# Two fused graph-attention layers: layer 0's softmax bound on ScalarE, its shift as a reduction, and another order of the mixed phase

## The chip, the cores and the metric

One core of a Trainium2 chip runs the whole program. The metric is the time of one execution on the device, in microseconds (us). A kernel's time is the median of several executions. Profiles come from one execution of their own.

## The reference, cut to what matters

For each of 16 graphs with 512 nodes and 256 channels, layer 0 is one attention head with a 0/1 mask and layer 1 has eight heads whose logits get the logarithm of the clipped adjacency:

```python
# layer 0
q = x @ Wq + bq;  k = x @ Wk + bk
scores = where(adj == 0, -1e18, (q @ k.T) / sqrt(256))
attn   = where(adj == 0, 0, softmax(scores))
x = layernorm(x + (attn @ x) @ Wc) * gamma + beta
# layer 1, heads of 32 channels
logits = q_h @ k_h.T / sqrt(32) + log(clip(adj, 1e-8))
x = layernorm(x + concat_h(softmax(logits) @ v_h) @ Wo.T + bo) * gamma + beta
```

## The kernel before, in words

Each graph goes through a front (layer 0 and layer 1's projections), a back (layer 1's attention) and a tail (output projection, residual, layernorm, store). The program runs phases: in phase i the front of graph i+1, the back of graph i and the tail of graph i-1 are mixed. There are 18 phases: one with a front only, one with front and back, fourteen full ones (a hardware loop), one with back and tail, one with the tail alone. In layer 1 a "quad" is four heads by 128 keys; a back has eight quads of two pairs each.

The order inside a phase is a list written out by hand, `SCHEDULE` for the mixed phases (`FIRST` and `LAST` for the ends). Every engine walks the same list and does its own share of each named stage (function `follow`), so PE, VectorE (`dve`), ScalarE (`act`) and GpSimd (`pool`) each have a strict queue, and semaphores tie them. SyncE issues all transfers in an order of its own, with waits on VectorE's and GpSimd's progress.

Stages that the change and the prediction touch:

- `max0` (L650, L652, L989): upper bounds of layer 0's scores on PE; VectorE takes the negated maximum of 512 columns per row tile, into `mx0`.
- `u` (L608, L826): PE forms x @ Wc and, in one more column, what the key's bias adds to each row's scores; ScalarE copies it to `U`. `floor` (L995) adds a large constant to that column for the four row tiles, on VectorE, into `floor0`: a bound for rows without any neighbour.
- `shift0` (L1000): VectorE takes the smaller of `mx0` and `floor0`, 4 numbers per partition, into `nm0`. ScalarE spreads it to `NM0` (L832), and PE adds it in the first `scores0` (L667).
- `reciprocal`, `normalise` (L1057), `high_output` (L862, ScalarE), `low_output` (L1061, VectorE): turn the sums of one group of four heads into the high and low parts `OTH`, `OTL` of the attention's output. With index 1 they belong to the graph before. `project` (L770) on PE multiplies them by Wo; its sixth matmul is the first that reads `OTL` of group 1. `project` on VectorE (L1070) adds the residual; `stats1`, `norm1` (L1086) and `output` make the layernorm.
- `scores1` (L719, L847, L1144): PE's scores of a pair, ScalarE's exponential, and GpSimd's multiplication by the clipped adjacency (the "mask"; a few are on VectorE, stages `mask`, L985). `values1`, `denominators1` (L742) sum a quad on PE after its masks.
- `residual` (L1127, L1129): two GpSimd operations that prepare `res` from `xn`; `norm0` (L1044) on VectorE overwrites `xn` and waits for them, `transpose` on PE (L685) waits for `norm0`.
- `max1` (L698, L1005): one matmul and one VectorE reduction per head and row tile. `clip` (L973), `bias` (L977): VectorE makes the clipped adjacency and the mask of missing edges.

The four `MISC` banks of PSUM are given out in the list's order to the stages of `MISC_DRAIN`; a fill waits until the use four places before it has been drained. `skip_back` and `skip_front` are places in that count with no work.

Of the kernel before, what the change touches and what calls it, by code (L numbers as in the profile page):

```python
# [32 lines left out]
ALU = mybir.AluOpType  # L33
ACT = mybir.ActivationFunctionType
AX = mybir.AxisListType

P = 128
# [13 lines left out]
class Phase:  # L51
# [20 lines left out]

SCHEDULE = [
    ("reciprocal", 1, 0), ("max1", 1, 0), ("split", 0), ("split", 1), ("reciprocal", 1, 1),
# [13 lines left out]
    ("reciprocal", 0, 0), ("reciprocal", 0, 1), ("scores1", 6, 0), ("transpose", 0), ("scores1", 6, 1),  # L88
    ("transpose", 1), ("reciprocal", 0, 2), ("reciprocal", 0, 3), ("values1", 5), ("scores1", 7, 0),
# [6 lines left out]
]  # L96

LAST = [
# [129 lines left out]
def two_layer_graph_attention(nc, x, x_t, adj_t, wq0, wk0, wc0, wq1_t, wk1_t, wv1_t, wo1_t,  # L228
                              channel_cols, channel_rows, out):
    B, N, D = x.shape  # L230
    T = N // P
# [15 lines left out]
    with ExitStack() as ctx:  # L247
        def sb(name, shape, dt=F32):
            return ctx.enter_context(nc.sbuf_tensor(name, shape, dt))
# [4 lines left out]
        def sem(name):  # L254
            return ctx.enter_context(nc.semaphore(name))
# [27 lines left out]
        absent = sb("absent", [P, 1])  # L283
        Q0H, Q0L = (sb(n, [P, C, N], F32R) for n in ("Q0H", "Q0L"))
        U = sb("U", [P, T, 1 + D + 2])
        mx0 = sb("mx0", [P, T])
        floor0 = sb("floor0", [P, T])
        nm0 = sb("nm0", [P, T])
        floor_bias = sb("floor_bias", [P, 1])
        NM0 = sb("NM0", [P, T, P], F32R)  # L290
# [72 lines left out]
        floor0_ready = sem("floor0_ready")  # L363
        nm0_ready = sem("nm0_ready")
# [20 lines left out]
        sums_out = sem("sums_out")  # L385
# [16 lines left out]
        def misc_bank(ph, *stage):  # L402
            return MISC[misc.bank(ph, *stage)]

        def wait_drained(eng, ph, *stage):

            e = MISC_DRAIN[stage[0]]
            eng.wait_ge(misc_drained[e], misc.count(ph, e, *stage))

        def wait_filled(eng, ph, *stage):  # L410
            eng.wait_ge(misc_filled, misc.count(ph, "fill", *stage))
# [376 lines left out]
        def _(act):  # L788
# [23 lines left out]
            def hi(ph, stage, c, dst, bias):  # L812

                wait_filled(act, ph, stage, c)
                act.activation(dst[:, c, :], misc_bank(ph, stage, c)[:], ACT.Identity,
                               bias=cols[:, bias, c:c + 1]).then_inc(hi_written, 1)
# [7 lines left out]
            def context_rows(ph, t):  # L824
                wait_filled(act, ph, "u", t)
                act.copy(U[:, t, 1:1 + D + 2], misc_bank(ph, "u", t)[:, 0:D + 2]).then_inc(misc_drained["act"], 1)  # L826

            def shift0(ph):

                act.wait_ge(nm0_ready, ph.j + 1)  # L830
                for t in range(T):
                    act.activation(NM0[:, t, :], ident[:], ACT.Identity, scale=nm0[:, t:t + 1]).then_inc(nm0_spread, 1)  # L832
# [31 lines left out]
            def xn_high(ph, c):  # L864
# [4 lines left out]
            do = {  # L869
                "prepare": prepare, "split": split,  # L870
                "q0": lambda ph, c: hi(ph, "q0", c, Q0H, BQ0),
                "u": context_rows, "shift0": shift0,
                "scores0": exp0, "transpose": xn_high,
                "q1": lambda ph, c: hi(ph, "q1", c, Q1H, BQ1),
                "k1": lambda ph, c: hi(ph, "k1", c, K1H, BK1),
# [8 lines left out]
        def _(dve):  # L884
# [76 lines left out]
            def lo(ph, stage, c, dst, hi_part, bias):  # L961

                wait_high(ph, stage, c)
                dve.scalar_tensor_tensor(out=dst[:, c, :], in0=misc_bank(ph, stage, c)[:],  # L964
                                         scalar=cols[:, bias, c:c + 1], in1=hi_part[:, c, :].bitcast(F32),
                                         op0=ALU.add, op1=ALU.subtract).then_inc(misc_drained["dve"], 1)
# [19 lines left out]

            def max0(ph, t):
                wait_filled(dve, ph, "max0", t)
                dve.tensor_reduce(mx0[:, t:t + 1], misc_bank(ph, "max0", t)[:], AX.X,  # L989
                                  ALU.max, negate=True).then_inc(misc_drained["dve"], 1)  # L990

            def floor(ph):

                wait_drained(dve, ph, "u", T - 1)
                dve.tensor_scalar(floor0[:], U[:, :, 1 + D], floor_bias[:, 0:1], None, ALU.add).then_inc(floor0_ready, 1)  # L995

            def shift0(ph):
                wait_drained(dve, ph, "max0", T - 1)
                dve.wait_ge(floor0_ready, ph.j + 1)
                dve.tensor_tensor(nm0[:], mx0[:], floor0[:], ALU.min).then_inc(nm0_ready, 1)  # L1000

            def max1(ph, g, n):
                t, h = divmod(n, PER_GROUP)
# [79 lines left out]
            def norm1(ph):  # L1083
# [5 lines left out]
            do = {  # L1089
                "prepare": prepare, "split": split, "clip": clip, "bias": bias,  # L1090
                "q0": lambda ph, c: lo(ph, "q0", c, Q0L, Q0H, BQ0),
                "mask": mask, "max0": max0, "floor": floor, "shift0": shift0, "context0": context0,
                "stats0": stats0, "norm0": norm0, "stats1": stats1,
                "transpose": xn_low,
                "q1": lambda ph, c: lo(ph, "q1", c, Q1L, Q1H, BQ1),
# [98 lines left out]
```

## Time and profile before

| | us |
|---|---|
| median of 3 runs (lowest, highest) | 1311.65 (1310.07, 1313.34) |
| the profiled execution, its span | 1313.88, 1312.1 |
| PE busy | 1188.1 (91%) |
| VectorE busy | 1019.7 (78%) |
| GpSimd busy | 733.7 (56%) |
| ScalarE busy | 522.1 (40%) |

Busy times add up an engine's instructions; the idle rest of an engine is waiting for another one or for its own next instruction. In the timeline an instruction's duration includes time in which it has been started but is held up. Matmuls overlap each other, so their starts say more than their ends. Successive VectorE instructions overlap by 0.08 us in the records, and successive GpSimd ones by 0.04.

### The profile page before, as it was taken

How to read it: one execution, taken by the hardware profiler on the slowest of the kernel's cores; microseconds unless marked ns; L12 is line 12 of the kernel's file. 1: busy time of each engine (PE TensorE's matmuls, PEld its weight loads, DVE VectorE, ACT ScalarE, POOL GpSimd, SP SyncE). 2: the span in 40 equal slices, each digit the busy share in tenths (PEclk: the TensorE clock that was granted, in tenths of full speed). 3: DMA queues.
4: the chain of work that ended last, by engine and by line, in shares of the span. 5: the costliest groups of instructions: out<-in, count | busy, mean ns of one | idle time of the engine just before them, and what ended most of it. 6: DMA issues, size and time to landing. Idle time of an engine off the chain costs nothing.

```text
span 1312.1 us, 21162 instructions
## 1 busy us (share of the span) xinstructions
PE 1188.1 (91%) x6474; PEld 697.3 (53%) x6474; DVE 1019.7 (78%) x1751; ACT 522.1 (40%) x1004; POOL 733.7 (56%) x352
## 2 busy tenths in 40 slices
PE   6889998989989898998989899998989989898883
PEld 5655464645546464554646456464655546465432
DVE  4365887978788787878879787887978788797874
ACT  2233444444344444434444443444444344444421
POOL 0016376483747648374774837467483746748362
PEclk8889999999999999999999999999999999999877
DMA  3041321404132140413214041321504132150310
GB/s 121 1 129 33 101 77 39 123 16 136 40 98 78 37 123 16 132 44 98 76 35 128 16 132 45 94 71 39 134 16 126 51 94 66 42 134 16 80 33 16
DMA packets 69652, 94.67 MB, mean 72 GB/s; under 512 B 14081, under 2 KB 32769, under 8 KB 69634
## 3 DMA queue, kind: packets, MB, share of 16 engines
q1 hardware_dynamic: 69634, 94.44, 25.7%
q8 instruction: 10, 0.16, 0.1%
q14 instruction: 8, 0.07, 0.0%
HBM read 35.40 MB, written 8.39 MB: 33 GB/s over the span
## 4 chain that ended last, share of the span: by engine, by line
PE 47%; POOL 20%; DVE 15%; issue 12%; ACT 4%; DVEq 1%; DMA 1%; POOLq 0%; ACTq 0%; SPq 0%
POOL PR L1144 10%; PE misc L598 9%; PE scores L719 6%; DVE mx L1005 5%; PE misc L698 5%; PE values L742 4%; PE denominators L742 4%; DVE xn L1044 4%; PE misc L608 3%; POOL z L1156 3%; PE misc L663 3%; PE misc L650 3%; POOL res L1127 2%; PE misc L620 2%; PE values L770 2%
## 5 line engine op out<-in xcount | busy, mean ns | idle before, releaser
L1144 POOL TENSOR_TENSOR PR<-PR,CLIP 128x1024 f32<-128x1024 f32 x217 | 529.6, 2458 | 453.9 <-ACT PR L847 453.9
L847 ACT ACTIVATE PR<-scores 128x512 f32<-128x512 f32 x512 | 278.5, 598 | 329.2 <-PE scores L719 321.3
L1005 DVE TENSOR_REDUCE mx<-misc 128x1 f32<-128x512 f32 x512 | 321.3, 680 | 52.6 <-PE misc L698 50.8
L719 PE MATMUL scores<-QS,KS 97*128 97x512 f32 x512 | 199.9, 469 | 8.6 <-issue 3.4
L742 PE MATMUL values<-PR,V 128*32 128x512 f32 x1024 | 135.6, 614 | 21.0 <-ACT sums_v L856 10.7
L719 PEld LDWEIGHTS scores<-QS,KS 97*128 97x128 f32 x512 | 89.9, 198 | 91.6 <-ACT PR L847 53.4
L698 PE MATMUL misc<-K1H,Q1H 32*128 32x512 f32 x512 | 128.0, 502 | 7.8 <-DVE K1L L964 4.0
L742 PE MATMUL denominators<-PR,ones 128*32 128x512 f32 x1024 | 134.2, 607 | 0.6 <-DVE z L1070 0.3
L1052 DVE RECIPROCAL sums_w<-sums_w 128x128 f32<-128x128 f32 x128 | 114.1, 925 | 10.0 <-issue 5.2
L676 PE MATMUL misc<-U,P 128*128 128x257 f32 x512 | 120.2, 383 | 0.0
L698 PEld LDWEIGHTS misc<-K1H,Q1H 32*128 32x128 f32 x512 | 54.9, 184 | 118.9 <-DVE mx L1005 50.0
L676 PEld LDWEIGHTS misc<-U,P 128*128 128x128 f32 x512 | 95.6, 189 | 17.7 <-issue 3.5
L1133 POOL TENSOR_TENSOR ve<-mv,eps 128x4 f32<-128x4 f32 x32 | 19.8, 617 | 104.7 <-DVE mv L1036 59.2
L836 ACT ACTIVATE P<-misc 128x512 f32<-128x512 f32 x64 | 38.3, 598 | 84.8 <-PE misc L668 84.8
L1044 DVE TENSOR_SCALAR xn<-X,mv,rstd 128x256 f32<-128x256 f32 x64 | 52.7, 887 | 19.4 <-POOL rstd L1135 19.4
L742 PEld LDWEIGHTS values<-PR,V 128*32 128x32 f32 x1024 | 23.7, 109 | 78.7 <-issue 37.1
L1086 DVE TENSOR_SCALAR z<-z,mv,rstd 128x256 f32<-128x256 f32 x64 | 51.9, 874 | 13.8 <-POOL rstd L1135 13.8
L1021 DVE TENSOR_SCALAR den<-misc 128x1 f32<-128x1 f32 x64 | 10.1, 158 | 67.3 <-PE misc L676 67.3
L663 PE MATMUL misc<-Q0H,XTH 128*128 128x512 f32 x128 | 57.6, 450 | 3.8 <-ACT P L836 3.8
L985 DVE TENSOR_TENSOR PR<-PR,CLIP 128x1024 f32<-128x1024 f32 x39 | 51.1, 1316 | 3.3 <-ACT PR L847 2.9
L989 DVE TENSOR_REDUCE mx<-misc 128x1 f32<-128x512 f32 x64 | 43.8, 685 | 9.7 <-PE misc L652 8.4
L663 PE MATMUL misc<-Q0L,XTH 128*128 128x512 f32 x128 | 50.9, 397 | 0.0
(159 smaller groups left out, 1996.4 us busy)
## 6 DMA issues: line engine op xcount, KB each, us to landing
ADJ<-adj_t SPq DMA_DIRECT2D x16, 1024.0 KB, 6.0
QS<-Q1H SPq DMA_DIRECT2D x256, 64.0 KB, 2.0
KS<-K1H SPq DMA_DIRECT2D x256, 64.0 KB, 2.0
P<-x_t SPq DMA_DIRECT2D x16, 512.0 KB, 3.8
X<-x SPq DMA_DIRECT2D x16, 512.0 KB, 3.7
QS<-Q1L SPq DMA_DIRECT2D x128, 64.0 KB, 2.0
KS<-K1L SPq DMA_DIRECT2D x128, 64.0 KB, 2.0
out<-z SPq DMA_DIRECT2D x16, 512.0 KB, 2.9
```

The lines of the kernel that those rows point to most:

```text
L598: mm = pe.matmul(bank[:], w[:, k, P * c:P * (c + 1)], s[:, k, :], start=(n == 0), stop=(n == len(terms) - 1))
L663: pe.matmul(bank[:], kk[:, c, rows_k], qq[:, c, :], start=(n == 0), stop=False)
L676: mm = pe.matmul(bank[:, 0:D + 1], P0[:, k, P * t:P * (t + 1)], U[:, k, 0:D + 1], start=(k == 0), stop=(k == T - 1))
L698: pe.matmul(bank[:], Q1H[part, g, P * t:P * (t + 1)], K1H[part, g, :], start=True, stop=True).then_inc(misc_filled, 1)
L719: pe.matmul(ST[n][:], KS[:, h, P * k:P * (k + 1)], QS[:, h, :], start=True, stop=True).then_inc(scores_filled, 1)
L742: mm = pe.matmul(bank[DK * h:DK * (h + 1), :], w, PR[quad % WEIGHT_BUFFERS][:, h, :], start=(k == 0), stop=(k == T - 1))
L847: act.activation(PR[quad % WEIGHT_BUFFERS][:, h, :], ST[n][:], ACT.Exp, scale=SCALE1).then_inc(exp_done, 1)
L1005: dve.tensor_reduce(mx1[:, g, h, t:t + 1], misc_bank(ph, "max1", g, n)[:], AX.X, ALU.max, negate=True).then_inc(misc_drained["dve"], 1)
L1044: dve.tensor_scalar(xn[:, t, :], X[:, t, :], mv0[:, t, 0:1], rstd0[:, t:t + 1], ALU.subtract, ALU.mult).then_inc(xn_ready, 1)
L1052: dve.reciprocal(sums_w[:, q], sums_w[:, q]).then_inc(back_step, 1)
L1086: dve.tensor_scalar(z[:, t, :], z[:, t, :], mv1[:, t, 0:1], rstd1[:, t:t + 1], ALU.subtract, ALU.mult).then_inc(zn_ready, 1)
L1144: pool.tensor_tensor(w, w, clipped, ALU.mult).then_inc(masked_pool, 1)
```

## The change

`floor` moves from VectorE to ScalarE. `mx0` and `floor0` become the two columns of one tile `bounds0`, and the shift is a `tensor_reduce` with minimum over them. The list `SCHEDULE` has a new order; `FIRST` and `LAST` stay. What is computed stays the same.

```diff
-        mx0 = sb("mx0", [P, T])
-        floor0 = sb("floor0", [P, T])
+        bounds0 = sb("bounds0", [P, T, 2])
+        MAXIMUM, FLOOR = 0, 1
@@ scalar engine
+            def floor(ph):
+                wait_drained(act, ph, "u", T - 1)
+                act.activation(bounds0[:, :, FLOOR], U[:, :, 1 + D], ACT.Identity,
+                               bias=floor_bias[:, 0:1]).then_inc(floor0_ready, 1)
@@ vector engine
-                dve.tensor_reduce(mx0[:, t:t + 1], misc_bank(ph, "max0", t)[:], AX.X,
+                dve.tensor_reduce(bounds0[:, t, MAXIMUM:MAXIMUM + 1], misc_bank(ph, "max0", t)[:], AX.X,
                                   ALU.max, negate=True).then_inc(misc_drained["dve"], 1)
-            def floor(ph):
-                wait_drained(dve, ph, "u", T - 1)
-                dve.tensor_scalar(floor0[:], U[:, :, 1 + D], floor_bias[:, 0:1], None, ALU.add).then_inc(floor0_ready, 1)
             def shift0(ph):
                 wait_drained(dve, ph, "max0", T - 1)
                 dve.wait_ge(floor0_ready, ph.j + 1)
-                dve.tensor_tensor(nm0[:], mx0[:], floor0[:], ALU.min).then_inc(nm0_ready, 1)
+                dve.tensor_reduce(nm0[:], bounds0[:], AX.X, ALU.min).then_inc(nm0_ready, 1)
@@ SCHEDULE, the parts that differ, old
-    ("q0", 1), ("bias",), ("scores1", 0, 0), ("u", 0), ("scores1", 0, 1), ("u", 1), ("scores1", 1, 0), ("u", 2),
-    ("reciprocal", 1, 3), ("max0", 0), ("max0", 1), ("scores1", 1, 1), ("normalise", 1), ("max0", 2), ("u", 3),
-    ("skip_back",), ("floor",), ("low_output", 1), ("max1", 1, 2), ("max1", 1, 3), ("max1", 1, 4),
-    ("high_output", 1), ("max0", 3), ("project",), ("scores1", 2, 0), ("skip_back",), ("max1", 1, 5),
-    ("shift0",), ("stats1",), ("max1", 1, 6), ...
-    ("denominators1", 1), ("values1", 2), ("max1", 1, 14), ("max1", 1, 15), ("residual",), ("scores1", 3, 1),
-    ("context0", 0), ("mrow1", 1), ...
-    ("k1", 0), ("normalise", 0), ("q1", 1), ("max1", 0, 0), ("max1", 0, 1), ("max1", 0, 2),
-    ("denominators1", 5), ("max1", 0, 3), ("scores1", 7, 1), ("values1", 6), ("max1", 0, 4), ... ("max1", 0, 7),
-    ("denominators1", 6), ("clip",), ("k1", 1), ("denominators1", 7), ("max1", 0, 8), ("max1", 0, 9),
-    ("max1", 0, 10), ("high_output", 0), ("values1", 7), ("low_output", 0), ("max1", 0, 11), ("max1", 0, 12),
-    ("sums_out", 1), ("v", 0), ...
@@ new
+    ("q0", 1), ("scores1", 0, 0), ("u", 0), ("scores1", 0, 1), ("skip_back",), ("u", 1), ("scores1", 1, 0),
+    ("u", 2), ("bias",), ("reciprocal", 1, 3), ("max0", 0), ("skip_back",), ("max0", 1), ("normalise", 1),
+    ("high_output", 1), ("scores1", 1, 1), ("max0", 2), ("max0", 3), ("max1", 1, 2), ("max1", 1, 3), ("u", 3),
+    ("low_output", 1), ("max1", 1, 4), ("project",), ("scores1", 2, 0), ("stats1",), ("floor",),
+    ("max1", 1, 5), ("shift0",), ("max1", 1, 6), ...
+    ("denominators1", 1), ("scores1", 3, 1), ("max1", 1, 14), ("max1", 1, 15), ("values1", 2), ("skip_front",),
+    ("context0", 0), ("mrow1", 1), ("residual",), ...
+    ("k1", 0), ("q1", 1), ("max1", 0, 0), ("max1", 0, 1), ("max1", 0, 2), ("denominators1", 5), ("values1", 6),
+    ("max1", 0, 3), ("scores1", 7, 1), ("normalise", 0), ("max1", 0, 4), ... ("max1", 0, 7),
+    ("denominators1", 6), ("max1", 0, 8), ("clip",), ("k1", 1), ("high_output", 0), ("max1", 0, 9),
+    ("low_output", 0), ("max1", 0, 10), ("values1", 7), ("denominators1", 7), ("max1", 0, 11), ("max1", 0, 12),
+    ("v", 0), ("sums_out", 1), ...
```

## Rows read from the trace of the kernel before

**Rows 1.** Page, section 1: busy us (share of the span) xinstructions.

```profile
PE 1188.1 (91%) x6474; PEld 697.3 (53%) x6474; DVE 1019.7 (78%) x1751; ACT 522.1 (40%) x1004; POOL 733.7 (56%) x352
```

**Rows 2.** Page, section 4: the chain that ended last, by engine.

```profile
PE 47%; POOL 20%; DVE 15%; issue 12%; ACT 4%; DVEq 1%; DMA 1%; POOLq 0%; ACTq 0%; SPq 0%
```

**Rows 3.** Busy time of two neighbouring mixed phases; start:end, length, then engines, clock.

```profile
542.95:619.11 76.16, 71.22 (x401) 41.56 (x401) 62.64 (x107) 32.19 (x63) 46.94 (x22) 1.00 0.27 76
619.11:696.49 77.38, 72.50 (x401) 42.65 (x401) 62.76 (x107) 32.20 (x63) 46.89 (x22) 0.98 0.27 74
```

**Rows 4.** Timeline, VectorE, one mixed phase: start, us, what [idle before <-releaser].

```profile
555.27 0.68 DVE L989 TENSOR_REDUCE mx<-misc 128x1 f32<-128x512 f32 x1
556.40 1.22 DVE L995 TENSOR_SCALAR floor<-U,floor_bias 128x4 f32<-128x4 f32 x1 [0.45 <-ACT U L826]
557.53 0.68 DVE L1061 TENSOR_TENSOR OTL<-sums_v,OTH 128x512 fp32r<-128x512 f32 x1
558.14 1.87 DVE L1005 TENSOR_REDUCE mx<-misc 128x1 f32<-128x512 f32 x3
...
562.35 2.28 DVE L1000 TENSOR_TENSOR nm<-mx,floor 128x4 f32<-128x4 f32 x1
```

**Rows 5.** Timeline, GpSimd's masks in the same phase, one narrow window each.

```profile
554.76 2.83 POOL L1144 TENSOR_TENSOR PR<-PR,CLIP 128x1024 f32<-128x1024 f32 x1
...
557.55 2.91 POOL L1144 TENSOR_TENSOR PR<-PR,CLIP 128x1024 f32<-128x1024 f32 x1
...
562.24 2.37 POOL L1144 TENSOR_TENSOR PR<-PR,CLIP 128x1024 f32<-128x1024 f32 x1 [1.78 <-ACT PR L847]
```

**Rows 6.** The shift's line over the run: duration ns min/median/max, first and last start.

```profile
L1000 DVE TENSOR_TENSOR nm<-mx,floor x16: 162/2280/2287, 32.0 to 1177.2; 128x4 f32<-128x4 f32 x16
```

**Rows 7.** Timeline, ScalarE, same phase.

```profile
554.28 1.09 ACT L847 ACTIVATE PR<-scores 128x512 f32<-128x512 f32 x2 [1.36 <-PE scores L719]
555.99 0.37 ACT L826 COPY U<-misc 128x258 f32<-128x258 f32 x1 [0.62 <-PE misc L608]
```

**Rows 8.** Waits of the whole run: us in total, times, longest us.

```profile
PEld misc L667 <- ACT NM L832: 7.3, 15, 1.3
...
PE values L742 <- POOL PR L1144: 10.2, 14, 0.8
```

**Rows 9.** Timeline, PE, same phase, project and the next stage.

```profile
558.18 0.47 PE L770 MATMUL values<-Wo_high,OTL 128*128 128x256 f32 x2
...
560.64 0.64 PE L719 MATMUL scores<-QS,KS 97*128 97x512 f32 x2
```

**Rows 10.** Timeline, VectorE, the phase without a front.

```profile
1244.44 1.78 DVE L1061 TENSOR_TENSOR OTL<-sums_v,OTH 128x512 fp32r<-128x512 f32 x1
...
1261.44 1.77 DVE L985 TENSOR_TENSOR PR<-PR,CLIP 128x1024 f32<-128x1024 f32 x1
...
1263.34 3.16 DVE L985 TENSOR_TENSOR PR<-PR,CLIP 128x1024 f32<-128x1024 f32 x1
```

**Rows 11.** Timeline, GpSimd, the phase without a front.

```profile
1243.31 2.36 POOL L1144 TENSOR_TENSOR PR<-PR,CLIP 128x1024 f32<-128x1024 f32 x1 [2.70 <-ACT PR L847]
...
1262.08 3.33 POOL L1127 TENSOR_TENSOR res<-xn,spread 128x1024 f32<-128x1024 f32 x1
```

**Rows 12.** Timeline, PE, the transposes of a later phase.

```profile
827.54 0.43 PE L685 MATMUL misc<-ident,xn 128*128 128x128 f32 x1 [1.69 <-DVE xn L1044]
```

**Rows 13.** Timeline, VectorE, the tail of the phase.

```profile
604.42 0.68 DVE L1057 TENSOR_TENSOR sums_v<-sums_v,sums_w 128x512 f32<-128x512 f32 x1
...
608.68 2.49 DVE L1005 TENSOR_REDUCE mx<-misc 128x1 f32<-128x512 f32 x4 [0.39 <-PE misc L698]
```

**Rows 14.** PE's busy time and granted clock in stretches of two phases.

```profile
619.42:622.83 3.41, 2.56 (x8) 1.00 0.36 88
622.84:626.25 3.41, 3.41 (x9) 0.50 0.44 108
...
827.63:831.04 3.41, 3.41 (x15) 0.50 0.00 0
```

More of the change, by code:

```diff
@@ L74 @@
     ("reciprocal", 1, 0), ("max1", 1, 0), ("split", 0), ("split", 1), ("reciprocal", 1, 1),
[13 rows of a table removed]
-    ("reciprocal", 0, 0), ("reciprocal", 0, 1), ("scores1", 6, 0), ("transpose", 0), ("scores1", 6, 1),
-    ("transpose", 1), ("reciprocal", 0, 2), ("reciprocal", 0, 3), ("values1", 5), ("scores1", 7, 0),
[6 rows of a table removed]
+    ("reciprocal", 1, 2), ("max1", 1, 1), ("q0", 0), ("q0", 1), ("scores1", 0, 0), ("u", 0),
+    ("scores1", 0, 1), ("skip_back",), ("u", 1), ("scores1", 1, 0), ("u", 2), ("bias",),
+    ("reciprocal", 1, 3), ("max0", 0), ("skip_back",), ("max0", 1), ("normalise", 1), ("high_output", 1),
[11 rows of a table added]
+    ("transpose", 0), ("scores1", 6, 1), ("transpose", 1), ("reciprocal", 0, 2), ("reciprocal", 0, 3),
[6 rows of a table added]
 ]
@@ L871, in _ @@
                 "q0": lambda ph, c: hi(ph, "q0", c, Q0H, BQ0),
-                "u": context_rows, "shift0": shift0,
+                "u": context_rows, "floor": floor, "shift0": shift0,
                 "scores0": exp0, "transpose": xn_high,
@@ L1091, in _ @@
                 "q0": lambda ph, c: lo(ph, "q0", c, Q0L, Q0H, BQ0),
-                "mask": mask, "max0": max0, "floor": floor, "shift0": shift0, "context0": context0,
+                "mask": mask, "max0": max0, "shift0": shift0, "context0": context0,
                 "stats0": stats0, "norm0": norm0, "stats1": stats1,
```

35 rows, old and new, of the table SCHEDULE are left out of this document.

## The prediction

> **What bounds the kernel now.** I read the busy shares of the page first, then the chain of waits, then the length of two neighbouring mixed phases, then one phase engine by engine in the timeline. TensorE is busy 91% of the span, VectorE 78% [rows 1]. Nearly half of the chain that ended last is PE [rows 2]. A mixed phase takes 76.2 to 77.4 us and holds 71.2 to 72.5 us of PE work [rows 3]; fourteen of the eighteen phases are of this full kind. So time is won or lost only where PE, which works strictly in its listed order, waits. The work taken off VectorE counts only as far as a PE wait hangs on it. All positions below are those of the phase that begins at 542.95.
>
> **What the edit removes.** The bound costs 1.22 us and the shift 2.28 us on VectorE for four numbers per partition [rows 4]. The shift starts at 562.35, just behind a GpSimd mask of 562.24 to 564.61 [rows 5], and ends 0.02 us after it; the shortest of the 16 shifts took 162 ns [rows 6]. So the shift costs 2.1 us of waiting for GpSimd's running instruction, and the bound likewise: it begins at 556.40 and ends at 557.62, when the mask of 554.76 (2.83 us) is over at 557.59. ScalarE's new bound is a 128x4 activation; its nearest row is the copy of 0.37 us that precedes the bound now [rows 7]. It stands behind the weights of quad 2 and before the shift, where ScalarE has idle time, so I put it at nothing (bounds 0 and 0.4). The new reduction over pairs has 8 elements; nearest rows are the 162 ns of the free shift and 0.68 us for 512 elements, so 0.16. No row shows a reduction from SBUF beside a GpSimd mask; its upper bound is the present 2.28. The Trainium skill (SBUF — State Buffer, Who interferes with whom) says that a tensor_reduce never contends with GpSimd and a tensor_tensor with two SBUF inputs does; by it the shift takes the lower value, which is what I take from the rows anyway.
>
> VectorE so loses 3.3 us of waiting in each phase. What was PE's share? The weights load of the shift's matmul waited for ScalarE's NM, 7.3 us in 15 times, 0.49 on average [rows 8]; part of that would be idle time of the loader anyway. I take 0.3 per phase (bounds 0 and 0.5).
>
> **The order, front part.** PE's list is the same up to max0 2. Then the old one has u 3, max1 2 to 4, max0 3, project; the new one max0 3, max1 2, max1 3, u 3, max1 4, project. What decides is ("low_output", 1) on VectorE. Project's sixth matmul reads its result. Now it follows the bound directly: VectorE was already waiting when the mask ended at 557.59, so low_output ran at 557.53 to 558.21, GpSimd's next mask was held behind both (2.91 us instead of the 2.37 of the mask at 562.24), and project, whose first pair with OTL starts at 558.18, needs the result for the second of the pair at 558.30, just in time [rows 4, 5, 9].
>
> In the new order four reductions stand ahead of it. Max0 2 starts at 555.27; max0 3 ends on PE where u 3 ends its first part, so its reduction starts at about 555.97; three steps at 0.60 (three reductions take 1.87) bring low_output to the head at about 557.78. But by then nothing on VectorE has been waiting at 557.59, and GpSimd starts mask (1, 1) at 557.55 to 557.59. Its input is ready: the exponentials now stand behind high_output on ScalarE and slip from 554.28 to about 555.9 (1.09 long [rows 7]), ready at 557.0. So low_output comes some 0.2 us too late for the gap between two masks and waits for the whole of one.
>
> Do 0.2 us suffice? The last phase has this operation caught so: started at 1244.44 in a mask of 1243.31 to 1245.67, it ended at 1246.22, 0.55 after the mask [rows 10, 11]. And a VectorE mask that ended at 1263.21 let a waiting GpSimd operation (recorded from 1262.08) go; the next VectorE mask, begun at 1263.34, 0.13 later, was held until 1265.41 and took 3.16 us [rows 10, 11]. The present shift begins 0.11 after its mask and is held as well. So yes.
>
> Sum for the front: mask (1, 1) unheld 557.55 + 2.37 = 559.92, low_output done 0.55 later, 560.47, and PE goes on at 560.5. PE has started project earlier, at 556.9, does five matmuls and waits about 3.1 us. The remainder takes 560.64 - 558.30 = 2.34 [rows 9], so the next stage starts at 562.85 instead of 560.64: **+2.2 us**. Behind it z, statistics, one reduction and the shift follow on VectorE; the shift is ready at about 566.2, four NM activations end at 567.5, and PE wants them at 568.05: no further wait, so the 0.3 above stands as **-0.3**. If the reduction were held after all, it would end with mask (2, 0) at about 566.9, NM at 568.2: 0.15 worse. The held tile of norm1 goes (its mask now comes later than its four tiles), but nothing on PE waits for that.
>
> **Middle.** GpSimd now does mask (3, 1) before residual, not behind it. Values of quad 3 wait for that mask now, 10.2 us in 14 times, 0.73 each [rows 8]. With residual's two operations behind it this wait goes: **-0.7**. Next in line is PE's own work in front of it. Residual ends one mask (2.4 us) later than now, and norm0, which needs it, follows only after context 3, its statistics and a VectorE mask: covered by several us; uncovered it would cost at most that mask. The big stall of the phase, transpose waiting 1.7 us for the fourth tile of norm0, which a mask holds [rows 12], hangs on context 3 and quad 5, whose mutual order is unchanged; it stays.
>
> **Tail.** normalise 0 filled an idle gap of VectorE at 604.42 and now stands in the reductions [rows 13]: +0.6 on VectorE, of which the gap of 0.39 before max1 4 takes the larger part. max1 8 comes before clip, so k1 1 on PE waits for one more reduction (+0.4), v 0 starts 0.2 later; v 1 no longer waits for sums_out on ScalarE. At the end of the phase this nets **+0.1** (bounds -0.3 and +0.6). clip 0.7 later moves SyncE's load of ADJ and the stack transfers behind it by 0.2 to 0.3 us; the stacks' first reader has over 1 us to spare. The two skip_back and the moved skips only change banks; each new predecessor has drained by then. bias is in the same place of VectorE's own list.
>
> Per full phase 2.2 - 0.3 - 0.7 + 0.1 = +1.3, fourteen times: **+18 us**. The phase without a tail has no low_output 1 and gains about 0.6; the first and last lists are unchanged.
>
> **The clock.** From 619.42 on PE worked only 2.56 of 3.41 us, and the next stretch was granted 0.50 [rows 14]; that phase is 77.38 long instead of 76.16 [rows 3], 1.2 us more. After the transpose stall at 827.54 the clock fell to 0.50 too [rows 12, 14]; in most phases that same stall has full clock behind it. The new stall is 3.1 us against 1.7. I expect half speed (1.2 GHz) behind it in 11 or 12 of the 14 phases, at 1.2 each: **+14 us** (bounds 0 and 20). The Trainium skill (TensorE: Matmul & The Clock Gate, Why this matters for your kernels) warns of idle gaps between bursts of matmuls in the same sense; no run here yet shows it for this place.
>
> Total: 1313.9 for the profiled execution (span 1312.1) + 18 + 14 - 0.6 = 1345 for such an execution; it lay 2.2 above the median of the three runs, 1311.65, against which I get 1343. **Forecast 1344.**
>
> **Rivals.** (a) Held, but the clock stays up: 1311.65 + 18 = 1330. For it: the transpose stalls mostly pass without a drop. Chance 0.24. (b) The other side: low_output slips in before mask (1, 1), because VectorE is 0.2 us quicker than I count or GpSimd slower between two masks. It then ends at about 558.5, PE resumes there, +0.2 instead of +2.2: -0.7 per phase, 1302. It decides at 557.59. For it: only 0.2 us; against: the caught row with 0.13. Chance 0.14. (c) As (b), and norm0 comes clear of its mask by a shift of 0.3 us: another 1.7 per phase, 1278. Nothing in the order moves these against each other; 0.04. (d) The reduction is held as well: 1346, inside the forecast. Forecast (held, clock falls, 1336 to 1357) 0.50; worse than that, with two slow stretches per phase, 0.05; no visible difference 0.03.
>
> So faster by over 0.3% 0.18, within 0.3% (about what measurement can tell from nothing) 0.04, slower 0.78. The likeliest case alone spans 1336 to 1357; for 8 in 10 the range must take (a) and (b): 1300 to 1357.
>
> **What would show it.** Right: low_output 1 takes about 2.7 us in 14 phases, against 0.68 now [rows 4]; PE waits in project about 3 us for OTL; the wait of values for the mask is gone; the shift takes under 0.3 us and the bound is on ScalarE; slices with a lower PE clock become more. Wrong: low_output at 0.7 us, then the time falls to 1302; a shift above 2 us; a wait of values 3 that stays; or residual late before norm0.

## The result, and the profile after

| kernel | median of the runs, us (lowest, highest) | ratio to before (95% interval) |
|---|---|---|
| before | 1312.49 (1310.07, 1314.5) | |
| after | 1344.88 (1342.52, 1347.51) | 1.0248 (1.0219 to 1.0277) |

The change made the kernel slower by 32.4 us. The profiled execution of after took 1342.52 us, span 1340.7, against 1313.88 and 1312.1 before; these two differ by only 28.6, because after's profiled execution is its fastest and before's lies above its median. All after rows below are of the phase that begins at 553.77 unless another is named.

The page of after, busy times and the chain by engine, against [rows 1, 2]:

```profile
PE 1202.5 (90%) x6458; PEld 708.6 (53%) x6474; DVE 972.2 (73%) x1735; ACT 525.1 (39%) x1020; POOL 725.6 (54%) x352
...
issue 34%; POOL 31%; PE 17%; DVE 13%; ACT 3%; POOLq 1%; DMA 0%; DVEq 0%; SPq 0%; ACTq 0%
```

VectorE did 47.5 us less and the kernel still got slower. PE busy rose by 14.4 although its work is the same: matmuls at half clock are longer.

Three neighbouring mixed phases of after, with the columns of [rows 3]:

```profile
553.77:632.81 79.04, 72.92 (x400) 43.06 (x401) 59.44 (x107) 32.38 (x64) 46.31 (x22) 0.98 0.26 75
632.81:712.68 79.87, 74.15 (x399) 43.89 (x401) 59.38 (x107) 32.35 (x64) 46.34 (x22) 0.96 0.25 71
712.68:790.23 77.55, 71.41 (x400) 41.54 (x401) 59.42 (x107) 32.46 (x64) 46.30 (x22) 1.00 0.27 76
```

One stretch at half clock, two, and none (below such a stretch is also called a drop). The phase at full clock is 77.55, against 76.16 in [rows 3]. VectorE in the timeline of after, answering to [rows 4]; then GpSimd's masks (1, 0) and (1, 1) from narrow windows, answering to [rows 5]:

```profile
565.87 1.43 DVE L995 TENSOR_REDUCE bounds<-misc 128x1 f32<-128x512 f32 x2
567.21 1.28 DVE L1006 TENSOR_REDUCE mx<-misc 128x1 f32<-128x512 f32 x2
568.40 2.64 DVE L1062 TENSOR_TENSOR OTL<-sums_v,OTH 128x512 fp32r<-128x512 f32 x1
...
578.22 0.15 DVE L1001 TENSOR_REDUCE nm<-bounds 128x4 f32<-128x8 f32 x1
```

```profile
565.35 2.83 POOL L1145 TENSOR_TENSOR PR<-PR,CLIP 128x1024 f32<-128x1024 f32 x1
...
568.13 2.37 POOL L1145 TENSOR_TENSOR PR<-PR,CLIP 128x1024 f32<-128x1024 f32 x1
...
576.58 2.37 POOL L1145 TENSOR_TENSOR PR<-PR,CLIP 128x1024 f32<-128x1024 f32 x1 [6.08 <-ACT PR L853]
```

Low_output 1 starts 0.27 us after mask (1, 1) has started, and ends at 571.04, 0.54 after that mask's end at 570.50. In the fourteen full phases it starts 0.22 to 0.30 behind the mask's start and ends 0.55 behind its end each time. The shift lies wholly inside the mask of 576.58 and takes 0.15 us. The rule of the Trainium skill (SBUF — State Buffer, Who interferes with whom) that the prediction drew on, that a tensor_reduce does not contend with GpSimd, so has its row here.

PE in project, same phase, answering to [rows 9], then its granted clock in two stretches, as [rows 14]:

```profile
568.85 0.28 PE L770 MATMUL values<-Wo_high,OTL 128*128 128x256 f32 x1
571.10 0.39 PE L770 MATMUL values<-Wo_high,OTL 128*128 128x256 f32 x1 [1.97 <-DVE OTL L1062]
...
574.98 0.63 PE L719 MATMUL scores<-QS,KS 97*128 97x512 f32 x2
```

```profile
567.55:570.96 3.41, 1.58 (x9) 1.00 0.42 103
571.44:574.85 3.41, 3.41 (x18) 0.50 0.65 190
```

The records put the first OTL matmul at 568.85, ahead of its releaser's end; the weights of the next waited 2.2 us. After 1.58 busy us in a stretch of 3.41, PE was granted half speed, 1.2 GHz, and the rest of project ran at it. Waits of the whole run, answering to [rows 8]:

```profile
PE misc L685 <- DVE xn L1045: 29.2, 16, 3.8
PE values L770 <- DVE OTL L1062: 27.8, 14, 2.0
...
PEld misc L667 <- ACT NM L838: 1.4, 1, 1.4
```

The new wait for OTL stands there 14 times; the values' wait for a mask (10.2 us in 14 times) has left the list, and that of the shift's matmul fell from 15 times to 1.

Counted over the granted clock's stretches of the whole run: the fourteen full phases took 1075.6 us before and 1107.8 after. Half-speed stretches that begin in them:

| | begin at q0 (about +3 us) | behind project (+17 to +20) | behind the transposes (+55 to +58) | a phase without any |
|---|---|---|---|---|
| before | 6 | 0 | 2 | 76.06 to 76.16 us |
| after | 3 | 10 | 4 | 77.55 and 77.69 us |

### The profile page after: what moved, and what is told of

It reads as the page before. It is cut to its first block, busy times and chain, and to the rows that moved or that the text cites. A ratio compares the mean times of both kernels' runs of the same rounds, so it can differ in the third digit from the quotient of the medians.

```text
span 1340.7 us, 21132 instructions
## 1 busy us (share of the span) xinstructions
PE 1202.5 (90%) x6458; PEld 708.6 (53%) x6474; DVE 972.2 (73%) x1735; ACT 525.1 (39%) x1020; POOL 725.6 (54%) x352
## 4 chain that ended last, share of the span: by engine, by line
issue 34%; POOL 31%; PE 17%; DVE 13%; ACT 3%; POOLq 1%; DMA 0%; DVEq 0%; SPq 0%; ACTq 0%
POOL PR L1145 18%; PE misc L598 6%; DVE mx L1006 5%; DVE xn L1045 4%; POOL z L1157 3%; POOL res L1130 2%; POOL res L1128 2%; POOL rstd L1136 2%; POOL z L1159 2%; PE scores L719 2%; POOL ve L1134 1%; DVE CLIP L979 1%; PE values L742 1%; PE misc L676 1%; PE misc L663 1%
## 5 line engine op out<-in xcount | busy, mean ns | idle before, releaser
L1145 POOL TENSOR_TENSOR PR<-PR,CLIP 128x1024 f32<-128x1024 f32 x217 | 521.9, 2423 | 525.3 <-ACT PR L853 525.2
L1006 DVE TENSOR_REDUCE mx<-misc 128x1 f32<-128x512 f32 x512 | 323.3, 681 | 99.6 <-PE misc L698 99.2
L698 PE MATMUL misc<-K1H,Q1H 32*128 32x512 f32 x512 | 133.7, 503 | 9.3 <-DVE K1L L970 4.7
L742 PEld LDWEIGHTS denominators<-PR,ones 128*32 128x32 f32 x1024 | 25.1, 109 | 53.3 <-issue 50.8
L1062 DVE TENSOR_TENSOR OTL<-sums_v,OTH 128x512 fp32r<-128x512 f32 x32 | 50.6, 1580 | 1.4 <-ACT OTH L868 1.4
L995 DVE TENSOR_REDUCE bounds<-misc 128x1 f32<-128x512 f32 x64 | 44.1, 689 | 9.9 <-PE misc L652 8.0
```

The lines of the kernel that those rows point to most:

```text
L698: pe.matmul(bank[:], Q1H[part, g, P * t:P * (t + 1)], K1H[part, g, :], start=True, stop=True).then_inc(misc_filled, 1)
L742: mm = pe.matmul(bank[DK * h:DK * (h + 1), :], w, PR[quad % WEIGHT_BUFFERS][:, h, :], start=(k == 0), stop=(k == T - 1))
L1006: dve.tensor_reduce(mx1[:, g, h, t:t + 1], misc_bank(ph, "max1", g, n)[:], AX.X, ALU.max, negate=True).then_inc(misc_drained["dve"], 1)
L1145: pool.tensor_tensor(w, w, clipped, ALU.mult).then_inc(masked_pool, 1)
```

## The experiments

Each has its median, its ratio to before on the same chip with the 95% interval, and from its profile the length of a phase without half-speed stretch and the number of such stretches in the fourteen phases. The counts are of one profiled execution each.

**1 and 5: low_output one place earlier; the whole old front.**

```diff
-    ("max1", 1, 2), ("max1", 1, 3), ("u", 3), ("low_output", 1), ("max1", 1, 4), ("project",),
+    ("max1", 1, 2), ("low_output", 1), ("max1", 1, 3), ("u", 3), ("max1", 1, 4), ("project",),
```

Expected of the first:

> The changed kernel with low_output 1 one place earlier on VectorE (behind the second of the four reductions instead of the third of max1, so three steps of 0.60 become two); nothing else on any engine moves. Theory (held behind a mask): it then stands at VectorE's head about 0.35 us before mask (1, 0) ends, gets the gap, ends 0.55 us after that mask, and project does not wait. Per full phase the 2.2 us and about 0.8 drops of the clock at 1.2 us go, and PE's small waits between max1 3 and project of the old order are not there either: 1344.9 - 14 x 3.3 = about 1298, range 1290 to 1308. Rival (the loss lies in ScalarE's new order, in the middle or in the tail): above 1330.

Expected of the other, after's kernel with before's list up to `("max1", 1, 6)`:

> The changed kernel (edit included) with the old order up to the reduction max1 6, the new order behind it: only the middle and the tail of the new list are in it. The edit with the old list had phases of 75.08 us without a drop of the clock, of which 0.15 were the wait of values 3 for mask (3, 1). Theory (front order carries the loss; middle worth what is left of that wait, tail +0.1 to +0.3): phases of 75.0 to 75.3, time 1284 to 1294 depending on how many half-speed stretches fall in. Rival (middle or tail lose by themselves): above 1300.

Measured: 1294.30 us, 0.9853 (0.9838 to 0.9868), phase 75.27, 4 stretches; and 1294.70, 0.9863 (0.9849 to 0.9877), 75.24, 4. The first lies in its range, the second 0.7 above its own, with the phase as expected. Timeline of the first: VectorE, and the GpSimd mask (1, 0) beside it:

```profile
473.71 0.68 DVE L1006 TENSOR_REDUCE mx<-misc 128x1 f32<-128x512 f32 x1
474.30 0.96 DVE L1062 TENSOR_TENSOR OTL<-sums_v,OTH 128x512 fp32r<-128x512 f32 x1
```

```profile
471.85 2.86 POOL L1145 TENSOR_TENSOR PR<-PR,CLIP 128x1024 f32<-128x1024 f32 x1
```

Started 0.41 us before the mask's end at 474.71, the same instruction ends 0.55 after it and takes 0.96 instead of 2.64. One reduction's place, 0.6 us of VectorE, is worth 50.6 us of kernel: 2.28 per phase at full clock (77.55 - 75.27, so 31.9 in 14) and 13 fewer half-speed stretches. The rest of the new front is worth nothing (e5 equals e1).

**2: work put in PE's wait.** Twenty matmuls of operands already there, in front of project's own, into the bank that project then overwrites.

```diff
+                for _ in range(5):
+                    for n, (w, s, k) in enumerate(terms[:2 * C]):
+                        pe.matmul(PV[:, 0:D], s[:, k, 0:P], w[:, k, :], start=(n == 0), stop=(n == 2 * C - 1))
```

Expected:

> The changed kernel with 20 extra matmuls per project (the first four products of its first row tile, repeated five times, 20 x 0.12 = 2.4 us of PE work), in front of the wait for low_output. They lie inside the wait of about 3.1 us. Theory (the clock's share of the loss comes from PE's idleness there): PE is busy through the wait, the half-speed stretch behind project goes in the 10 phases that had one, 1344.9 - 10 x 1.2 = about 1333, range 1329 to 1338. Rival 1 (the half-speed stretches cost nothing that counts, or come from elsewhere): 1345. Rival 2 (PE was not really waiting, its work is the bound): 14 x 2.4 more, 1378.

Measured: 1339.21, 1.0191 (1.0173 to 1.0209), phase 77.70 (one such phase), 13 stretches; just above the range of 1329 to 1338. The wait for OTL is gone and no stretch lies behind project any more, so those ten hang on the stall. But 13 begin behind the transposes, where after had 4. One phase of it, then the stretches before and after its transpose stall of 1.70 us:

```profile
549.67:628.21 78.54, 74.78 (x420) 44.46 (x421) 59.48 (x107) 32.40 (x64) 46.38 (x22) 0.98 0.26 74
601.60:605.00 3.40, 1.70 (x15) 0.92 (x8) 3.40 (x5) 1.47 (x3) 2.94 (x2) 1.00 0.00 0
605.00:608.40 3.40, 3.40 (x16) 1.28 (x16) 3.11 (x5) 2.05 (x4) 3.40 (x2) 0.59 0.00 0
```

A drop there costs 78.54 - 77.70 = 0.84. That is why the time hardly fell: the drops moved.

**3 and 4: the edit alone, the order alone.** The new code with before's list; before's code with the new list.

Expected:

> The kernel before with only the edit: bound on ScalarE, shift as a reduction; the old order of stages. Theory (only what PE waited for the shift counts): 15 phases x 0.3 = 4.5 us less, 1308, range 1305 to 1311; low_output 1 still takes the gap after mask (1, 0), now waiting for it alone. Rival (VectorE is a bound, its 3.3 us less per phase count): 1312.5 - 15 x 3.3 = 1263.

Expected:

> The kernel before with only the new order: bound and shift as VectorE instructions with two inputs or two ports. Theory: low_output 1 is held as in the changed kernel; besides, the bound now stands beside mask (2, 0) and is held to its end, the shift comes behind it and a reduction, about 1.4 us later than the reduction gets there, of which some 0.7 to 1.1 reach PE: 1344.9 + 14 x 0.9 = 1358, range 1350 to 1366. Rival (the edit is worth only 0.3 us per phase in either order): 1349. Rival (the loss comes from the edit, not from the order): below 1320.

Measured: 1284.18, 0.9774 (0.9756 to 0.9792), phase 75.08, no stretch at all; and 1363.97, 1.0376 (1.0360 to 1.0392), every phase with a stretch, 23 in all. The edit is a gain of 30 us; the 1284 lies well outside the range of 1305 to 1311. The order costs 50 us without the edit and 61 with it, the former inside its range of 1350 to 1366. Of the order alone, waits, then the lines of the bound and of the shift over the run: low_output is held as in after. The bound is held by a mask, 1.33 to 1.52 us in the fourteen phases. The shift behind it is not held there (0.15 us), but comes later, and now makes the scores' matmul wait as well.

```profile
PE values L770 <- DVE OTL L1061: 27.9, 14, 2.0
...
PE misc L667 <- ACT NM L832: 7.8, 15, 0.9
```

```profile
L995 DVE TENSOR_SCALAR floor<-U,floor_bias x16: 228/1426/1521, 30.8 to 1230.6; 128x4 f32<-128x4 f32 x16
...
L1000 DVE TENSOR_TENSOR nm<-mx,floor x16: 145/146/1807, 31.1 to 1232.6; 128x4 f32<-128x4 f32 x16
```

For the edit alone I had expected 1308. One phase of it in the columns of [rows 3], then norm1's line over the run (ns, shortest/median/longest) in before and in the edit alone, then waits of before and of the edit alone:

```profile
532.30:607.39 75.09, 70.82 (x400) 41.48 (x401) 57.41 (x106) 32.50 (x64) 46.81 (x22) 1.00 0.27 77
```

```profile
L1086 DVE TENSOR_SCALAR z<-z,mv,rstd x64: 401/411/2549, 184.4 to 1303.5; 128x256 f32<-128x256 f32 x64
```

```profile
L1087 DVE TENSOR_SCALAR z<-z,mv,rstd x64: 405/407/417, 179.6 to 1273.8; 128x256 f32<-128x256 f32 x64
```

```profile
POOL z L1156 <- DVE z L1086: 10.7, 16, 1.5
```

```profile
POOL z L1157 <- DVE z L1087: 3.0, 2, 1.5
...
PE values L742 <- POOL PR L1145: 1.5, 10, 0.2
```

With the shift 2.1 us shorter, norm1 comes clear of the mask that held the third of its four tiles (2.52 to 2.55 us in all fourteen phases of before). GpSimd, which waited for norm1 with `output`, gets through it, mask (3, 0), residual and mask (3, 1) earlier: that last mask ends at +41.67 of the phase of 532.30, against +42.63 in the phase of 542.95 before. The values of quad 3 wait 1.5 us in the run instead of 10.2, which is 0.62 per phase; the loader's wait for NM fell from 7.3 us to 1.4, which is at most 0.42. The phase is 76.12 - 75.08 = 1.04 shorter. This chain is read off the traces; no run moves norm1 alone. Fourteen phases took 1051.0 us, 24.6 less than before: 14.6 by this, and the other 10 is the clock, eight stretches less.

**7: the new middle alone**, in before's code and list. Other entries of its list also moved, but in no engine's own order.

```diff
-    ("values1", 2), ("max1", 1, 14), ("max1", 1, 15), ("residual",), ("scores1", 3, 1), ("context0", 0), ("mrow1", 1),
+    ("scores1", 3, 1), ("max1", 1, 14), ("max1", 1, 15), ("values1", 2), ("skip_front",), ("context0", 0), ("mrow1", 1), ("residual",),
```

Expected:

> The kernel before with only the middle of the new order (scores 3, 1 earlier, residual behind mask (3, 1), values 6 and what follows as before); old code for bound and shift, old front and tail. Theory: the wait of values 3 for the mask goes, 0.73 us in 15 phases: 1313.7 - 11 = about 1303, range 1297 to 1308, with the number of half-speed stretches as the uncertainty. Rival (another wait takes its place): 1313.

Measured: 1306.31, 0.9962 (0.9945 to 0.9978), phase 75.67, 10 stretches. The time is in its range. The wait for the mask is gone, but the phase gains 0.45 and not 0.73. PE's timeline of before, and of this kernel, from the same place:

```profile
345.16 1.92 PE L742 MATMUL denominators<-PR,ones 128*32 128x512 f32 x16
346.90 1.04 PE L742 MATMUL values<-PR,V 128*32 128x512 f32 x8
...
350.70 0.39 PE L703 MATMUL misc<-ident,mx 128*16 128x128 f32 x2
```

```profile
421.59 1.92 PE L742 MATMUL denominators<-PR,ones 128*32 128x512 f32 x16
...
424.54 1.07 PE L742 MATMUL values<-PR,V 128*32 128x512 f32 x8
...
427.47 0.39 PE L703 MATMUL misc<-ident,mx 128*16 128x128 f32 x2
```

The same matmuls take 5.54 us before and 5.88 here, though PE waits for nothing in either. Directly behind the denominators the values have the same shape as what precedes them; parted from them they and their neighbours lose about 0.1 us at each change of shape. This is read off the rows; no run isolates it.

**8: added PE work in the edit alone.** Four matmuls more per project.

```diff
+                for n, (w, s, k) in enumerate(terms[:2 * C]):
+                    pe.matmul(PV[:, 0:D], s[:, k, 0:P], w[:, k, :], start=(n == 0), stop=(n == 2 * C - 1))
```

Expected:

> The edit with the old list, and four more matmuls (0.49 us of PE work) per project. The edit alone ran all its mixed phases without a half-speed stretch, 75.08 us each. Theory 1 (that was partly the luck of an alignment which hardly moved from phase to phase): the added work makes 14 x 0.49 = 7 us, and stretches at half speed come back in 4 to 8 phases at 1.2 each: 1296 to 1301. Theory 2 (the stretches went because the stalls behind them went): only the 7 us, 1291.

Measured: 1299.33, 0.9904 (0.9890 to 0.9919), phase 75.53, 4 stretches. That is in the range of theory 1. Of the 15 us over the edit alone the work is 6.3 (0.45 a phase), the stretches that came back, with no stall added, are 4.8, and 3.8 fall outside the fourteen phases. So the edit alone's freedom from them is partly how its phases happened to lie in time.

**9 and 10: the same slip in the old order.** In the edit alone, low_output 1 behind `("max1", 1, 3)`, and behind `("max1", 1, 4)`.

Expected:

> The edit with the old list, low_output 1 two reductions later on VectorE (behind max1 3); nothing else moves. It then reaches VectorE's head about 0.06 us after mask (1, 1) is recorded as started and 0.02 after the mask before has ended (14.53 against 14.47 and 14.51 in the edit's phase). Theory: that is late enough, it is held for a whole mask, ends at 17.4 instead of 15.06, PE goes on 2.2 us later: phases of 77.3 without a drop, and with drops behind project in most phases about 1325, range 1312 to 1332. Rival (below 0.1 us it still slips in): 1284 to 1290.

Expected:

> The same with three reductions ahead of low_output 1 (behind max1 4), which reaches the head 0.66 us after mask (1, 1) has started. Theory (the whole loss of the changed kernel is this hold, in whatever list it stands, and when in the mask it begins does not matter): low_output ends at the same 17.4, same loss as for two later if that one is held: phases of 77.3, about 1325, range 1312 to 1332. Rival (the old list has slack that takes it): 1284 to 1295.

Measured: 1344.23, 1.0233 (1.0212 to 1.0254), 17 stretches; and 1341.42, 1.0220 (1.0199 to 1.0240), 18. Both lie above the range of 1312 to 1332. The fourteen phases took 1106.7 and 1108.0 us, against 1051.0 in the edit alone: 14 x 2.28 = 32 is the hold as experiment 1 prices it, and the other 24 and 25 are left for the stretches, which I had taken as fewer and cheaper; no phase was without one. VectorE and the mask in 9:

```profile
568.51 2.79 DVE L1062 TENSOR_TENSOR OTL<-sums_v,OTH 128x512 fp32r<-128x512 f32 x1
```

```profile
568.38 2.37 POOL L1145 TENSOR_TENSOR PR<-PR,CLIP 128x1024 f32<-128x1024 f32 x1
```

and in 10:

```profile
567.20 2.19 DVE L1062 TENSOR_TENSOR OTL<-sums_v,OTH 128x512 fp32r<-128x512 f32 x1
```

```profile
566.47 2.36 POOL L1145 TENSOR_TENSOR PR<-PR,CLIP 128x1024 f32<-128x1024 f32 x1
```

Recorded 0.13 us or 0.73 us after the mask's start, it ends 0.55 or 0.56 after the mask's end, and PE waits 28.3 us in 14 times in both. Over the fourteen phases the distance was 0.08 to 0.13 in 9 and 0.68 to 0.73 in 10, and the subtraction was held every time. Two places move the edit alone from 1284 to 1344: this one instruction's place gives a slowdown as large as the whole new order's.

**6 and 11: the next stall, and a faster kernel.** The edit alone with VectorE's mask (5, 0) behind norm0; then also values 5 behind scores (7, 0), and normalise 0 behind max1 0 3.

```diff
-    ("mask", 5, 0), ("values1", 4), ("scores1", 5, 1), ("denominators1", 4), ("norm0",),
+    ("values1", 4), ("scores1", 5, 1), ("denominators1", 4), ("norm0",), ("mask", 5, 0),
@@ 11 alone
-    ("values1", 5), ("scores1", 7, 0), ("q1", 0), ("k1", 0), ("normalise", 0), ("q1", 1),
+    ("scores1", 7, 0), ("values1", 5), ("q1", 0), ("k1", 0), ("q1", 1), [up to] ("max1", 0, 3), ("normalise", 0),
```

Expected:

> The edit with the old list, and VectorE's mask (5, 0) behind norm0 instead of in front of it. Now that mask holds GpSimd's addition of epsilon by about 0.9 us, so norm0 comes 0.76 us before mask (5, 1) and its fourth tile is held 2 us; transpose waits 1.7. Theory: norm0 starts 0.9 earlier, its four tiles (1.3 us) end before mask (5, 1) starts, the transposes do not wait; the next limit is values 5, which needs masks (5, 0) and (5, 1), the latter now held by the former for 0.8: 1.1 us less per phase, 1284.2 - 15 x 1.1 = 1268, range 1262 to 1276. Rival (what follows waits as long for the masks): 1284.

Expected:

> The edit with the old list and three moves that the traces point to: VectorE's mask (5, 0) behind norm0 (as before), values 5 behind scores (7, 0) on PE (it waited 0.64 us for mask (5, 1)), normalise 0 behind the reduction max1 3 of the first group (it was held 0.9 us by mask (7, 0), and PE waited 0.57 for the queue behind it). Theory: the kernel with the mask alone had phases of 74.5 without a drop; 0.6 and 0.4 go: 73.5, 1279.9 - 15 x 1.0 = about 1265, range 1258 to 1275. Rival (the waits only move, as one did when the mask alone was moved): 1276 to 1282.

Measured: 1279.94, 0.9765 (0.9742 to 0.9788), 3 stretches; and 1274.32, 0.9702 (0.9675 to 0.9730), phase 73.53 to 73.74, 5 stretches, the fastest of all. The first misses its range of 1262 to 1276, the second is at the upper end of its own. Waits of 6, then two of its source lines over the run; last the waits of 11:

```profile
PE values L742 <- POOL PR L1145: 10.4, 21, 0.7
PE misc L698 <- DVE Q1L L970: 8.6, 15, 0.7
```

```profile
L1058 DVE TENSOR_TENSOR sums_v<-sums_v,sums_w x32: 676/766/1649, 141.4 to 1259.5; 128x512 f32<-128x512 f32 x32
...
L1045 DVE TENSOR_SCALAR xn<-X,mv,rstd x64: 404/408/414, 57.9 to 1178.8; 128x256 f32<-128x256 f32 x64
```

```profile
PE misc L685 <- DVE xn L1045: 3.8, 1, 3.8
...
PE values L742 <- POOL PR L1145: 0.9, 6, 0.2
```

In 6 the held tile of norm0 and the transpose stall (29 us in the run) are gone, but values 5 now wait for a mask and normalise 0 is held by one (1.57 us). The phase is 74.5 us instead of 75.08, which is 8 us less in fourteen, and three half-speed stretches take back half. The 4 us that remain are not clear of noise against the edit alone (0.9765 and 0.9774, with overlapping intervals). In 11 the wait and the hold are gone, and that gain is clear of both.

## Why the prediction was right

The sign, the size and the mechanism came out; several terms around them were mis-sized, and one step was wrong.

- **Low_output 1 held.** Forecast: 0.2 us too late, ends 0.55 after the mask. Measured 0.22 to 0.30 and 0.55, in all 14 phases. At full clock the stage behind project starts at +19.68 (732.36 in the phase of 712.68) against +17.69, so +2.0 for the forecast +2.2. Experiment 1 puts the whole price at 2.28. The wait itself was mis-sized: 3.1 us forecast, 2.0 measured on PE and 2.2 on its loader, because PE reached project at +14.49 and not +13.95 and went on at +17.33 and not +17.55. Experiment 1's kernel does what rival (b) described (put at 1302, measured 1294), and experiment 9 bears out the step on which (b) was refused, that a lead of 0.13 suffices: 0.08 did.
- **Shift and bound.** 0.15 us (forecast 0.16), bound 0.30 on ScalarE (0.37 was the nearest row). The NM wait went, as forecast. Rival (d) is out.
- **Middle, -0.7.** The wait went, but the order costs PE 0.34: -0.45 by experiment 7. Mis-sized: PE's matmuls were counted as if their order cost nothing.
- **Tail, +0.1.** Experiment 5 against 3 (75.24 and 75.08) gives +0.16 for new middle and tail together with the edit in both. Of that the middle is -0.15 + 0.34, if experiment 7's term holds here, so the tail is about zero. Not measured by itself.
- **Per phase +1.3.** Measured 77.55 - 76.12 = 1.43, with the mean of the seven undisturbed phases before (1.57 with the other undisturbed phase after, 77.69): +20 us in fourteen. The experiments split it: edit -1.04, rest of the order +0.19, low_output's place +2.28. That these add up to 1.43 is no check, as each is a difference of neighbours in the chain before, 3, 1, after.
- **Clock, +14.** Predicted: 11 or 12 drops behind project at 1.2. Measured 10 at 79.04 - 77.55 = 1.5, so about +15; two more behind the transposes at 0.84 add 1.7, and three fewer at q0 at 1.2 (77.38 - 76.16, [rows 3]) take off 3.7: 13. The fourteen phases' 32.2 less the 20 above leave 12. The forecast had taken the drops of before as staying, and had argued from a stall of 3.1 us where it was 2.0.
- **The ends, -0.6.** They took 236.5 us of the span before and 232.9 after: -3.6. The phase without a front alone is 2.2 shorter (59.1, now 56.9), and I had looked only at the phase without a tail (0.5 shorter, forecast 0.6). Most of the 2.2 goes with the clock: until its last wait PE ran 27.3 us of that phase at half speed before and 23.9 after. The edit alone has 56.2 with 20.5, but experiment 5, with the same edit, has 59.8 with 27.3, and experiment 7, without it, 57.8 with 23.9.

That the total came within 1 us of the measured median is luck. The forecast's terms add up to 31.4; in the two profiled executions they are 20 + 12 - 3.6 = 28.6, and the medians differ by 32.4.

What failed is the step "the held tile of norm1 goes, but nothing on PE waits for that". In the old order the values of quad 3 do, through GpSimd's queue, and with it the edit's own worth was 30 us where I had counted a few. The forecast came out because in after the error has no room to show: the new middle removes the same wait of the values in another way, and the gain by the clock is undone behind project. The step on the transposes ("it stays") held: 29.2 us against 29.1.

**What stays open.** Why the transpose stall of 1.7 us brings half speed in 2 phases of before, in 4 of after, in 13 of experiment 2, and in none of the edit alone; and why the stall in project does not in 4 of 14. The Trainium skill (TensorE: Matmul & The Clock Gate, Why this matters for your kernels) warns of idle gaps between bursts; the rows agree as far as the stretches behind project and behind the transposes follow a stall, but most of these stalls before the change pass without one. The drops at q0 have no such difference in front of them either: the prediction pointed at the 2.56 busy us of 3.41 ahead of one [rows 14], but the same place of the phases of 542.95 and 696.49, which have no drop, is no busier:

```profile
619.42:622.83 3.41, 2.56 (x8) 1.00 0.36 88
543.26:546.67 3.41, 2.55 (x8) 1.00 0.36 87
696.80:700.21 3.41, 2.55 (x8) 1.00 0.36 87
```

So how busy PE was in such a stretch does not by itself tell whether a drop follows. How many drops a variant gets could be counted only afterwards.

## What to carry to other kernels

Where VectorE and GpSimd work side by side, time every VectorE instruction with two inputs, or `tensor_scalar`, that a PE stage hangs on against the boundaries of GpSimd's long ones (here the bound, norm0 and norm1, all `tensor_scalar`, were held like low_output and the shift; the reductions were not): to arrive just before a boundary costs up to the rest of the running one, to arrive just after costs a whole one. Moving reductions in front of it is not free, though each takes 0.6 us. And test an edit and a reordering apart: here the one gained 30 us and the other lost 61 on top of it, and the result shows only their sum.

## What the runs showed of the hardware that was not expected

- 0.13 us between the recorded starts is enough for GpSimd to be first and the VectorE subtraction to take 2.79 us (experiment 9; in other phases of it 0.08 was enough). With VectorE waiting, the held 128x512 subtraction ends 0.54 to 0.56 us behind the mask, whether it arrived 0.41 before the mask's end, or 0.13, 0.27 or 0.73 after its start.
- A stall of 2 us in a stretch can cost more than itself: half speed behind it adds 1.5 us behind project, where 18 matmuls follow in a row, and behind the transposes, after a stall of 1.7 us, 0.84.
- 0.45 us of added PE work per phase brought four half-speed stretches into a kernel whose profiled execution had none in these phases (experiment 8).
